# RWKV attention and a mixture of experts on one core: value halves in slot 3, receptance mixes ahead of the gate, the first projection ahead of a product

## The reference

```python
shifted = pad(hidden, one step)[:, :-1]
key   = hidden * mk + shifted * (1 - mk)        # value, receptance alike
k, v, r = key @ Wk, value @ Wv, sigmoid(rec @ Wr)
mfo = max(mx, k_t + tf)                          # per channel, over the tokens
out = (exp(mx - mfo) * num + exp(k_t + tf - mfo) * v_t) / (the same with den)
num, den, mx = decayed by td = -exp(time_decay), plus the token's own share
x = layernorm(x + (r * out) @ Wo)
logits = x @ router_w.T; gate = softmax(logits) kept at its top 2 of 8
x = layernorm(x + sum_e gate_e * (silu(x @ down_e) @ up_e))
```

## Time and profile before

| | us |
|---|---|
| median of 3 runs (480.91 to 482.7) | 481.06 |
| the profiled execution's own time | 481.16 |
| its span, first to last instruction | 479.0 |

### The profile page before, as it was taken

The page is one execution under the profiler, slowest core; times in us unless marked ns, Lnnn a source line. Parts: engine busy times, 40 slices in busy tenths (PEclk is TensorE's granted clock), DMA queues, the critical chain, the costliest instruction groups (busy, mean ns, idle before and its releaser), DMA issues. The chain is left out here.

```text
span 479.0 us, 6524 instructions
## 1 busy us (share of the span) xinstructions
PE 459.9 (96%) x1930; PEld 329.7 (69%) x1930; DVE 413.5 (86%) x620; ACT 351.5 (73%) x792; POOL 289.0 (60%) x279
## 2 busy tenths in 40 slices
PE   8999899999999999999999999999999999999993
PEld 3444557776788777878778777887778775777461
DVE  6998979697989979998799988999799987785676
ACT  1677665765788698876888788876888868647675
POOL 2454784667647888369846688269864693321315
PEclk9999899999999999999999999999999999999998
DMA  8503320022000042001320042100420042300015
GB/s 251 191 1 119 95 74 1 19 92 89 1 1 0 2 141 95 29 0 61 117 89 0 1 132 70 64 0 23 134 88 22 1 133 90 131 0 1 0 45 219
DMA packets 20675, 31.41 MB, mean 66 GB/s; under 512 B 2080, under 2 KB 7200, under 8 KB 20640
## 3 DMA queue, kind: packets, MB, share of 16 engines
q1 hardware_dynamic: 20640, 31.00, 19.8%
HBM read 22.60 MB, written 8.39 MB: 65 GB/s over the span
## 5 line engine op out<-in xcount | busy, mean ns | idle before, releaser
L554 ACT ACTIVATE PR<-PR 128x512 f32<-128x512 f32 x128 | 74.3, 580 | 39.0 <-DVE PR L836 16.9
L1119 POOL TENSOR_SCALAR NM<-SUM,RS 128x1 f32<-128x1 f32 x30 | 8.1, 271 | 121.5 <-ACT RS L554 121.4
L1113 POOL TENSOR_TENSOR DQ<-DEN,EX 128x512 f32<-128x512 f32 x32 | 41.3, 1291 | 32.3 <-DVE DEN L807 32.3
L861 DVE SCALAR_TENSOR_TENSOR KT<-D,VEC,XT 128x512 f32<-128x512 f32 x57 | 54.0, 983 | 2.6 <-POOL KL L1097 2.6
L317 PE MATMUL PV<-VH,WVH 128*128 128x512 f32 x112 | 49.3, 441 | 2.1 <-DVE NU L831 2.0
L321 PE MATMUL PR<-RL,WRH 128*128 128x512 f32 x112 | 45.5, 407 | 3.2 <-POOL RL L1097 3.2
L317 PE MATMUL PK<-KH,WKH 128*128 128x512 f32 x112 | 48.5, 433 | 0.0
L807 DVE TENSOR_TENSOR_SCAN DEN<-PK,EX 128x512 f32<-128x512 f32 x32 | 39.0, 1220 | 9.9 <-ACT EX L554 7.5
L317 PE MATMUL PR<-RH,WRH 128*128 128x512 f32 x112 | 44.3, 395 | 0.6 <-DVE RW L848 0.6
L321 PE MATMUL PV<-VL,WVH 128*128 128x512 f32 x112 | 44.7, 399 | 0.0
L318 PE MATMUL PV<-VH,WVL 128*128 128x512 f32 x112 | 44.4, 396 | 0.0
(11 more groups left out here) (227 smaller groups left out, 1257.3 us busy)
## 6 DMA issues: line engine op xcount, KB each, us to landing
XT<-in_xt SPq DMA_DIRECT2D x32, 256.0 KB, 3.4
XN<-in_x SPq DMA_DIRECT2D x28, 256.0 KB, 2.6
out<-XN SPq DMA_DIRECT2D x28, 256.0 KB, 2.0
X1T<-in_wo SPq DMA_DIRECT2D x1, 1024.0 KB, 5.1
KT<-in_wo SPq DMA_DIRECT2D x4, 256.0 KB, 2.7
XT<-in_x SPq DMA_DIRECT2D x4, 256.0 KB, 4.4
out<-XT SPq DMA_DIRECT2D x4, 256.0 KB, 2.4
X1T<-in_wk SPq DMA_DIRECT2D x2, 256.0 KB, 5.0
```

The lines of the kernel that those rows point to most:

```text
L554: eng.activation(*a, **k).then_inc(q[s], 1)
L861: eng.scalar_tensor_tensor(out=full(b, which, c), in0=D[:, c, :], scalar=VEC[:, 2 + which, c:c + 1], in1=XT[:, c, 0:T], op0=ALU.mult, op1= ...
L1113: eng.tensor_tensor(DQ[:, :], DEN[:, 0:T], EX[:, 1, :], ALU.add).then_inc(q["e"], 1)
L1119: eng.tensor_scalar(NM1[:, col(t)], total, RS1[:, col(t)], scale, ALU.mult, ALU.mult)\
```

## The change

Five pieces of code move; no instruction is added or taken away, and no buffer changes.

```diff
@@ tensor
                 if 0 < s < U - 1:
                     key(s + 1)
+                if s == C:
+                    project(0)
                 rec(s)
-                if j == 0:
+                if j == 0 and b > 1:
                     for t in now[:1]:
                         project(t)
@@ scalar
                 if j == 3 and batch(b + 1):
-                    highs(b + 1, 1)
+                    highs(b + 1, 1, range(2, C))
...
                 for t in now[:1] if j < 3 and 1 < b < LAST else []:
                     halve(t + 1)
+                if j == 2 and batch(b + 1):
+                    highs(b + 1, 1, range(2))
@@ vector
+                if j == 3 and b:
+                    mixes(b + 1, 2, 0)
-                if 2 * C <= s < C * LAST:
+                if 8 <= s < C * LAST:
                     gate(s)
                 if s < U - 1:
                     scan_max(s + 1)
                     lead(s + 1)
...
                 if j == 3 and b:
-                    mixes(b + 1, 2, 0, 1)
-                if not 2 * C <= s < C * LAST:
+                    mixes(b + 1, 2, 1)
+                if not 8 <= s < C * LAST:
                     gate(s)
...
                 if j == 3:
-                    mixes(b + 1, 2, *((2,) if b else (0, 1, 2)))
+                    mixes(b + 1, 2, *((2, 3) if b else (0, 1, 2)))
...
                 if j == 3:
-                    mixes(b + 1, 2, 3)
+                    if b == 0:
+                        mixes(b + 1, 2, 3)
@@ gpsimd
-                if C <= s < 2 * C - 1:
+                if C <= s < 2 * C - 2:
                     low_weights(2, s - C + 1)
...
                 if j == 2 and batch(b + 1):
                     lows(b + 1, 0)
+                if s == 2 * C - 2:
+                    low_weights(2, C - 1)
                 if j == 3 and batch(b + 1):
-                    lows(b + 1, 1)
+                    lows(b + 1, 1, range(2, C))
...
+                if j == 2 and batch(b + 1):
+                    lows(b + 1, 1, range(2))
```

## The result

| | before | after |
|---|---|---|
| median, us | 481.28 (480.91 to 482.7, 4 runs) | 476.22 (476.04 to 476.57, 4 runs) |
| ratio, with its 95% interval | | 0.989 (0.9869 to 0.9912) |
| the profiled execution's own time, us | 481.16 | 476.57 |
| its span, us | 479.0 | 474.6 |

The changed kernel is faster by 5.1 us, 1.1%. The forecast was 476.5.

What follows compares the result with a forecast made beforehand. TensorE bounds slots 4 to 6 in part; a ring of VectorE, ScalarE and GpSimd paces slots 7 to 27. Slots 4 to 8 give -3.4 us, five later batches -1.3: 481.16 - 4.7 = 476.5 us, range 473 to 481.

Steps and rivals of the forecast that it cites:

- Slot 4: project(0) ahead of rec(4), once: `weigh(4)` slips 1.1 us and slot 5 starts 0.6 us late; +0.6 us.
- the ring: VectorE, ScalarE and GpSimd pacing slots 7 to 27; in slots 11, 15, 19, 23, 27 RH 3 gains: -0.26 us each, -1.3 together.
- Slot 6: Weight block moved behind the four KL on GpSimd, once, shortening VectorE's wait for KL 0; -1.27 us.
- Slots 7 and 8: Moved mixes make RH earlier, once: DEN of slot 8 at 115.4, not 119.32, -3.9 us before giving back 0.5.
- the whole front: Slots 4 to 8 together: -3.4 us, with bounds of -1 and -4.
- The giving back in slot 8: A turned tile from TensorE holds ScalarE in slot 8, giving back 0.5 us.
- XN goes first: First rival: XN holds the port ahead of mix 1, RH 1 0.52 us later, +0.26 a batch; 479.6 us, chance 0.25.
- RH's wait for D in slot 7: Sign that the forecast is right: this wait in slot 7 is near zero twice.
- The sign against the root: If ScalarE waits for TensorE anywhere from 126 to 395 us, TensorE sets the pace there.
- The front gives little: Rival: TensorE's products hold slots 7 and 8, so slots 4 to 8 yield 0 to -1; 480.5 us, chance 0.13.
- The gate's delay: Rival: DQ behind two VL delays gate and mix 1 by 1.7 us, 1.4 lost a batch; 485.0 us, chance 0.05.
- More than 0.26: Rival: later batches gain more, until TensorE's work bounds after about 1 us a batch; 472.8 us, chance 0.12.

Runs made afterwards that it cites:

- e5: The changed kernel with value halves VH and VL 0 and 1 put back into the batch's last slot; 476.84 us, ratio 0.9897.
- e8: The changed kernel with receptance mix 1 also ahead of the gate, behind mix 0; 478.15 us, ratio 0.9925.
- e11: The changed kernel with the two moved value halves ahead of their slot's spread and norm instead of behind; 478.85 us, ratio 0.9962.
- e3: The kernel before with only value halves VH and VL 0 and 1 moved to slot j = 2; 483.81 us, ratio 1.0044.
- e1: The kernel before with only project(0) moved ahead of rec(4) on TensorE; 481.44 us, ratio 0.9993.
- e2: The kernel before with only the last receptance weight block moved behind slot 6's four KL on GpSimd; 479.96 us, ratio 0.9968.
- e6: The changed kernel with receptance mix 3 put back behind `weigh`; 480.06 us, ratio 0.9964.
- e4: The kernel before with only the mixes moved: mix 0 ahead of the gate, mix 3 ahead of `weigh`; 477.46 us, ratio 0.9906.
- e7: The changed kernel with GpSimd's second norm ahead of the last VL in batches 2 to 6; 479.48 us, ratio 0.9948.
- e10: The changed kernel with spread ahead of the hidden-score copy in the first slot of batches 2 to 7; 479.02 us, ratio 0.9953.
- e9: The changed kernel with the last WRL weight block computed in slot 5 instead of behind slot 6's KL; 476.83 us, ratio 0.991.

## Why the prediction was right, step by step

**The total.** Forecast 476.5, measured 476.22. The sum was -4.7; the medians give -5.1, and the profile -5.3 with the opening taken off, of which the opening took 0.83 back in the profiled execution. That forecast and median lie within 0.3 us is in part luck: slot 4's loss was put 0.6 too high and the ring's gain 0.2 too high, and the 481.16 that it was counted from is 0.12 under the median of before in this comparison.

**Slot 4, forecast +0.6, measured 0.** The working was right for the execution that it was read from and wrong for this one, and the difference is the granted clock. In the profile of before it was 0.66 from 55 to 60 us, behind TensorE's wait of 1.98 us for NU, and the forecast took the rows as they stood (project(0)'s eight instructions were to "end at 65.3"). In the profile of after the clock stayed at 1.00, TensorE came to project(0) some 1.6 us sooner, and rec(4) reached its last product as RL 3 came (16.5 us behind DEN(3)) and not 1.3 us behind it. e5, e8 and e11 have project(0) first and the dip; e8 runs the same instructions as after until slot 7. All times are starts in us behind DEN(3):

| kernel | clock, 55 to 60 us | project(0) | last product of rec(4) | weigh(4) | DEN(5) | DEN(7) |
|---|---|---|---|---|---|---|
| before | 0.66 | 16.96 | 16.62 | 21.04 | 24.83 | 52.41 |
| after | 1.00 | 10.31 | 16.58 | 21.01 | 24.84 | 51.02 |
| e8 | 0.66 | 11.90 | 17.86 | 22.18 | 25.38 | 51.60 |
| e5 | 0.66 | 11.89 | 17.85 | 22.17 | 25.37 | 51.59 |

With the dip `weigh(4)` slips by 1.1 us and the ring enters slot 5 0.55 late, which is what the prediction wrote (1.1 and 0.6). Without it rec(4) is "1.1 us later" only at its start; its end hangs on RL 3. So the step that failed is the unspoken one, that the clock of one execution would be that of the next. With project(0) behind rec(4) the dip costs nothing: e3 has it and e1 and e2 do not, and their slots differ from before's 52.41 only by each part's own effect (52.35, 52.35, 51.15). project(0) ahead of rec(4) uses up the slack that hides it. All four timed runs of after had a mean clock of 0.996; whether the dip would come in others is open.

**Slot 6, forecast -1.27, measured -1.26 alone** (e2) and -1.40 in VectorE's wait for KL.

**Slots 7 and 8.** Forecast together with the entry -3.4 for the whole front, measured -1.39 - 3.25 + 0.40 = -4.24. The length of slot 7 came out almost exactly: from DEN(7), forecast at 102.37 less the 0.66, to DEN(8) it was to be 13.69 us and was 13.70, and mix 1 was to be through 8.2 behind DEN(7) and was. That the bare times agree too, 110.04 (109.9) and 115.51 (115.4), is luck: the 0.83 that the opening added stands about where slot 4's 0.6 did not come. The giving back in slot 8 was 0.40 (0.5). What was missing is mostly slot 4's 0.6. That mix 3 is the greater part (2.2 of 3.25 us) was in the working as "because RH 3 waited 1.95 us for mix 3"; e6 shows it.

**The ring, forecast -0.26 five times, measured -1.06 over the ring, -0.22 a batch.** The steps held. Mix 0 ended 0.56 behind DQ (0.55). From the gate to mix 1 it is 2.51 us in after and was 4.20: 1.69 less, which is the 1.7 by which the gate was to come late, made good as forecast. Counted from DEN(15) the gate starts at 6.85 us and started at 5.15, and mix 1 starts at 9.36 and started at 9.34. RH 2 and 3 took 1.15, not 1.41: the 0.26. RH 2 starts 0.03 later (13.36 behind DEN(15), from 13.33), and that is what is missing of the 0.26.

**Luck in the ring.** That mix 1 took 0.76 us hangs on a race that the working could not call: it had XN ahead by 0.08 us. It came out ahead by 0.04, and the mix won five times of five. In e3, where XN led by 0.08 to 0.10 (over mix 0 there), the mix lost five times of five. At the lead that the working had, the first rival is what e3 shows.

**What sets the pace of the ring.** The prediction had TensorE follow and VectorE, ScalarE and GpSimd set the pace. The waits of ScalarE and VectorE in after, 126 to 391 us (the list has waits of 0.15 us and more), still name no TensorE:

```profile
ACT RH L556 <- DVE D L865: 20.5, 10, 2.6
ACT EX L556 <- DVE PK L804: 10.1, 14, 0.7
...
DVE PR L840 <- POOL DQ L1120: 6.9, 5, 1.4
DVE DEN L811 <- ACT EX L556: 4.8, 5, 1.0
```

The slot of the receptance mixes shows the link that the forecast priced. Times in us behind DEN(15); the batch is the mean of three, DEN(15) to DEN(27):

| kernel | RH 3 ends | DEN(16) starts | between | batch | batch less this slot |
|---|---|---|---|---|---|
| before | 14.74 | 15.83 | 1.09 | 55.25 | 39.42 |
| after | 14.51 | 15.61 | 1.10 | 55.03 | 39.42 |
| e3 | 15.25 | 16.34 | 1.09 | 55.74 | 39.40 |
| e4 | 14.50 | 15.59 | 1.09 | 54.99 | 39.40 |
| e6 | 14.75 | 15.84 | 1.09 | 55.28 | 39.44 |
| e7 | 15.02 | 16.12 | 1.10 | 55.55 | 39.43 |
| e8 | 14.72 | 15.81 | 1.09 | 55.24 | 39.43 |

DEN(16) follows the end of RH 3 by the same 1.09 to 1.10 us in all seven, the two exponentials, and what a kernel wins or loses in this slot is what its batch wins or loses. The other three slots keep their 39.4 us; what holds them none of these seven moved. TensorE's work of 54.3 us a batch is no argument for TensorE. An engine that runs the same instructions has the same work whether it leads or follows: ScalarE's batch less its waits is 45.7 to 45.9 us in the same seven kernels. And e10 went against it.

TensorE is close, though. In after ScalarE's copy of a turned tile starts at 230.22, 0.04 us behind the end of TensorE's turn (230.18), when ScalarE had been free since 230.09. Its next instruction waits 1.11 us for the gate, so this tenth costs nothing. In e8 that wait for TensorE is 0.46 to 0.48 us in each of four batches.

**The signs named in advance.** The batch of 55.03 us (55.0), mix 1 at 0.76 (0.75), DEN(8) at 115.51 (near 116), a gate of slot 15 that does not wait for DQ and a `weigh` that does not wait for PR all came. One did not: RH's wait for D in slot 7 was to be near zero twice, and was 0.66 and 2.30. The sign contradicted the working, which had RH 0 from 107.05 and mix 1 through at 109.9, some 2.2 us of waiting for RH 1; only the third wait, 1.95 for mix 3, is gone. The sign against the root, a wait of ScalarE for TensorE, did not come at the 0.15 us of the list.

**The rivals.** *XN goes first* is a true mechanism. It did not happen in the five batches of after, but it did in one batch of e5 and one of e10, and in all five of e3. Its price is 0.5 a batch (0.49 in e5), as was put down (0.52). *The front gives little* fell with e4: the mixes hold slot 7. In slot 4 a product can hold the ring, as the rows with the dip show, but ScalarE's waits for products (9.4 us) were no sign of the pace of slots 7 and 8. *The gate's delay* is real only without the mixes, and there it is 0.5 a batch (e3), not 1.4. *More than 0.26* did not happen; the limit that it named, TensorE's work about 1 us below the batch of before, was not reached (TensorE's waits in before are 0.93 us a batch).

## What to carry to other kernels

Look for an instruction whose inputs are ready but which stands in order behind one that waits for another engine: mix 3 behind `weigh` was the greater part of this change (2.2 us of slot 7 and 1.3 of the ring, after against e6). Time the parts of a change alone and the whole without each, since the same part (the value halves) costs 2.4 us in one order and nothing in the other. Of the five moves two carry the result, the mixes and the weight block; those two without the rest were not timed. Before pricing a wait from the rows of one execution, look at the granted clock of its stretch: a dip that the next execution lacked moved a term here from +0.6 to 0. That an engine's work and its waits add up to the batch tells nothing of who sets the pace; look for an interval between two instructions that stays the same while the batch changes. Before removing a visible wait, ask what stands one place behind it and who else reads what is pushed back: e9 removed a wait of 0.61 us and gained nothing, and e10 shortened one and made a longer one.

## What the runs showed of the hardware

**A race within some hundredths of a microsecond.** A mix on VectorE and the scaling XN on GpSimd that start together hold each other up, though no semaphore is between them: one takes its 0.76 us and the other 1.27. In e3, XN led by 0.08 to 0.10 us in five batches and won all five. In after, e4, e5, e6, e9 and e10, with five batches each, it led by 0.02 to 0.05, and the mix won 28 of 30. In before XN had been waiting behind mix 0 for 0.48 us, and mix 1 still passed it: 0.75, with XN at 1.71. A subtraction of two tensors on GpSimd is not passed so: between two mixes it gets its turn (in slot 15 of e8 VL is issued 0.60 us ahead of the end of the first mix, and the second mix takes 1.77 us and ends 0.55 behind VL). The Trainium skill (SBUF — State Buffer, section "Who interferes with whom") has it that whoever issues first holds the pair for the instruction. The rows of e3 and the subtractions agree; mix 1 of before does not, nor do the 28 near ties as their starts are recorded.

**The opening and the dips.** Ten identical matmuls at the start took 6.05 us in before, 7.18 in after and 6.39 in e3. What follows moves with them in the main: DEN(0) starts 10.8 to 11.1 us later than their length in thirteen of the fourteen profiles, and 11.7 in e11. The granted clock fell at 56 us in five of the fourteen profiles (before, e3, e5, e8, e11) and not in the other nine, behind the same wait of 1.96 to 1.98 us: 1.98 us for NU in before (first row below, then the matmuls a little later, with 0.43 between starts), 1.97 us in after, where it stayed at 1.00 and the starts 0.23 apart. 0.43 against 0.23 fits the lower of the two levels, 1.2 GHz against 2.4. The five with the dip are those whose opening took 6.04 to 6.39 us; in the nine without it the opening took 6.75 to 7.63. What ties the two together is not shown.

```profile
54.65 0.50 PE L317 MATMUL PV<-VH,WVH 128*128 128x512 f32 x1 [1.98 <-DVE NU L831]
...
56.54 0.63 PE L317 MATMUL PV<-VH,WVH 128*128 128x512 f32 x1
56.97 0.63 PE L318 MATMUL PV<-VH,WVL 128*128 128x512 f32 x1
```
